# One F tile in two halves around the last scores, and the last attention tile copied tile by tile

## The chip, the cores and the metric

The kernel runs on one core of a Trainium2 chip. The metric is the device time of one execution in microseconds (us), which covers the profiled span and a little around it. All sums below are made against one profiled execution and then carried over to the median of the runs.

## The reference

A gated cross-attention block with a feed-forward layer, in fp32, over 4 batches of 512 tokens of 512 channels. The attention is across the 16 heads of one token, not across tokens.

```python
def _L0_xattn_ref(q, k, v, Wq, bq, Wk, bk, Wv, bv, Wo, bo):
    Q = (q @ Wq.T + bq).reshape(bs, sl, H, HD)      # H = 16, HD = 32
    K = (k @ Wk.T + bk).reshape(bs, sl, H, HD)
    V = (v @ Wv.T + bv).reshape(bs, sl, H, HD)
    score = jnp.einsum('bshd,bsgd->bshg', Q, K)
    weight = jax.nn.softmax(score, axis=-1)
    attn = jnp.einsum('bshg,bsgd->bshd', weight, V).reshape(bs, sl, nf)
    return attn @ Wo.T + bo
...
x = x + jnp.tanh(g_xattn[0]) * _L0_xattn_ref(_layernorm(x, axis=-1), ctx_2048, ctx_2048, ...)
x = x + jnp.tanh(g_ffn[0]) * _L0_ffn_ref(_layernorm(x, axis=-1), ...)   # x @ (weight*scale).T + bias
```

## The kernel before, in words

The 2,048 tokens are cut into 8 chunks of 256 tokens (`CHUNKS`), a chunk into 2 tiles of 128 (`TILES`). Every engine runs its own list of steps, `steps(...)`: steps 0 and 1 written out, 2 to 5 in a loop, 6, 7 and 8 written out. What an engine does in a step, and in which order, is fixed by hand in `tensor_step`, `vector_step`, `scalar_step`, `pool_step` and `sync_step`; the engines meet only through semaphores, and each works through its own list in order. Work on chunk c is called by a letter: V(c), K(c), Q(c), O(c), F(c) are the five matrix layers, score(c) and attend(c) the two small attention products, and F(5,0) is tile 0 of F(5).

Each large product is made in three parts to keep fp32 precision: every operand is split into a high part (written by ScalarE, `high`, L663) and a low part (what is left, written by VectorE, `low`, L838), and `product` (L440) adds high by high, high by low and low by high, 4 matmuls each, so 12 for a tile. A layer tile therefore waits first for the high part and, 8 matmuls later, for the low part of its input.

The change is in step 7, the last one with a chunk to attend, and touches TensorE (PE) and VectorE (DVE):

- TensorE, `tensor_step(7)`: score(7) needs q_pad, which comes back from DRAM by DMA. Then F(5,0) into the bank `score_ps[0]`, once VectorE has transposed score(7) out of that bank (`s_turned`, L545). Then O(6), F(5,1), `turn_x2` of tile (6,0) into the bank `turn_ps[0]`, attend(7). In step 8 (`last_tensor_step`): F(6,0) with the turn of (6,1) inside it, O(7), F(6,1) with the turn of (7,0), F(7,0) with the turn of (7,1), F(7,1).
- VectorE, `vector_step(7)`: `scores_turn` (L911), `softmax_a` (L923, L926), then `last_softmax_step` (L1089): the low parts of attention tiles (6,0) and (6,1) (`attn_low`, L966), `f_residual(5,0)` (L981), `softmax_b` (L934 to L941), and for each tile of chunk 6 `o_residual` (L989), `second_stats` (L852 to L863), `second_apply` (L874). The last comes back to the list once GpSimd (POOL) has made `rstd` (L1133).
- The attention result of chunk 7 lies in `attn_ps`. ScalarE (`attn_copy`, L738) and VectorE (`attn_some`, L975) copy it to `attn_t`, each 4 pieces of tile 0 and 4 of tile 1. `attn_high(7,t)` on ScalarE (L663) waits for both halves of tile t and makes its high part; `attn_low(7,t)` on VectorE waits for that. O(7) on TensorE needs both.
- GpSimd after `rstd` of both tiles adds the bias row, `x2_bias` (L1150). SyncE (SP) stores a finished tile after its `f_residual` (`save_y`, L348), in the order of its own list.

Of the kernel before, what the change touches and what calls it, by code (L numbers as in the profile page):

```python
# [66 lines left out]
def gated_attention_kernel(nc, x, ctx_t, g_attn, g_ffn, wq_t, bq, wk_t, bk, wv_t, bv, wo_t, bo,  # L67
                           wf_t, scale, bf, v_scratch, out):
    stack = ExitStack()
    with stack:  # L70
# [172 lines left out]
        def final(c):  # L243
            return isinstance(c, int) and c == CHUNKS - 1

        def late_f(c):

            return isinstance(c, int) and c == CHUNKS - 3
# [13 lines left out]
        def f_banks(c, t):  # L262

            if final(c) and t == TILES - 1:
                return last_tile
            if isinstance(c, int) and c >= CHUNKS - 3:
                return ((score_ps[t], slice(0, D)),)
            return ((acc[t], slice(0, D)),)
# [163 lines left out]
        def _(pe):  # L432
# [59 lines left out]
            def turn_x2(c, prev, tiles=range(TILES)):  # L492
                for t in tiles:
                    pe.wait_ge(n_done[1], TILES * c + t + 1)
                    prev(t)
                    turn(x2_norm, x2_turned, t)
# [4 lines left out]
            def x2_read(c):  # L501
                return lambda t: pe.wait_ge(x2_lo, TILES * c + t + 1)
# [31 lines left out]
            def f_layer(c, prev, prev_c):  # L534
# [2 lines left out]
                    bank_free(prev, prev_c, t)  # L537
                rows_layer(x2_parts, "wf", f_mm, high_ready, lambda t: pe.wait_ge(x2_lo, TILES * c + t + 1))

            def late_f_tile(c, t, within=None):  # L540

                def high_ready(t):
                    pe.wait_ge(x2_hi, TILES * c + t + 1)
                    if late_f(c):
                        pe.wait_ge(s_turned, TILES * (CHUNKS - 1) + t + 1)  # L545
                    elif final(c) and t == TILES - 1:
                        pe.wait_ge(o_out, TILES * CHUNKS)
                        pe.wait_ge(at_hi, TILES * CHUNKS)
                    else:
                        pe.wait_ge(f_out, TILES * (c - 1) + t + 1)  # L550

                def low_ready(t):
                    if within:
                        within()
                    pe.wait_ge(x2_lo, TILES * c + t + 1)
                rows_layer(x2_parts, "wf", f_mm, high_ready, low_ready, lambda t: f_banks(c, t), (t,))

            def score(c):
                pe.wait_ge(q_moved, DMA * GROUPS * (c + 1))
                pe.wait_ge(k_laid, c + 1)  # L560
                reached(pe, s_turned, 2 * c)
                pe.sem_inc(pe_passed, 1)
                for o in range(EIGHTS):
                    for pair in range(PAIRS):
                        n = GT // 2 * (pair // 2) + ROW_TOK * o + 2 * (pair % 2)
                        for r in range(2):
                            half = slice(ROWS * r, ROWS * (r + 1))
                            last = pe.matmul(  # L568
                                score_ps[r][HD * pair:HD * (pair + 1), ROWS * o:ROWS * (o + 1)],
                                k_keys[half, n:n + 2].rearrange("p s g -> p (s g)"),  # L570
                                q_pad[half, :, :, :, n:n + 2].rearrange("p t q m s -> p (t q m) s"),
                                start=True, stop=True)
                            if o == EIGHTS - 1 and pair == PAIRS - 1:
                                last.then_inc(score_mm, 1)
# [39 lines left out]
            def tensor_step(i):  # L614
                if final(i - 1):
                    return last_tensor_step(i)
                score(i)
                if final(i):
                    late_f_tile(i - 2, 0)
                    o_layer(i - 1, "v", i)  # L620
                    late_f_tile(i - 2, 1)
                    turn_x2(i - 1, x2_read(i - 2), (0,))
                    attend(i)
                    return
                if first(i):
                    q_layer(1, blocks=(1,))
                    v_layer(1)
                elif first(i - 1):
                    k_layer(2, "v", 1)
                    pe.wait_ge(w_lo, pieces_to(WO, 1))  # L630
                    o_layer(0, "k", 2)
                    q_layer(2, "o", 0)
                else:
                    o_layer(i - 1, "f", i - 2)
                    k_layer(i + 1, "o", i - 1)
                    q_layer(i + 1)
                attend(i)
                if exists(i - 1):
                    turn_x2(i - 1, x1_read(i + 1))
                    v_layer(i + 1)  # L640
                if exists(i - 1) and not late_f(i - 1):
                    if not exists(i - 2):
                        pe.wait_ge(w_lo, pieces_to(WF, 1))
                    f_layer(i - 1, "v", i + 1)
                if exists(i + 2):
                    turn_x1(i + 2, x2_read(i - 1) if exists(i - 1) else x1_read(i + 1))

            def last_tensor_step(i):

                late_f_tile(i - 2, 0, lambda: turn_x2(i - 2, x2_read(i - 3), (1,)))  # L650
                o_layer(i - 1, "o", i - 2)
                late_f_tile(i - 2, 1, lambda: turn_x2(i - 1, x2_read(i - 2), (0,)))
                late_f_tile(i - 1, 0, lambda: turn_x2(i - 1, x2_read(i - 2), (1,)))
                late_f_tile(i - 1, 1)
# [180 lines left out]
        def _(dve):  # L835
# [127 lines left out]
            def attn_low(c, t):  # L963
                dve.wait_ge(at_hi, TILES * c + t + 1)
                n = slice(P * t, P * (t + 1))
                low(at_parts(c)[:, LO, :, n], attn_t[:, :, n], at_parts(c)[:, HI, :, n]).then_inc(at_lo, 1)  # L966
# [91 lines left out]
            def vector_step(i):  # L1058
                if first(i):
                    return first_step()  # L1060
                if first(i - 1):
                    return second_step()
                if final(i - 1):
                    return last_step(i)
                scores_turn(i)
                softmax_a(i)
                if final(i):
                    return last_softmax_step(i)
                o_residual(i - 1, 0)
                softmax_b(i)  # L1070
                o_residual(i - 1, 1)
                turned_lo(xa_parts, x1_hi, x1_lo, i + 1)
                spread_first(i)
                for t in range(TILES):
                    second_stats(i - 1, t)
                    second_apply(i - 1, t)
                if exists(i + 2):
                    norm_stats(0, x_norm, i + 2)
                    norm_apply(0, x_norm, x_norm, i + 2)
                turned_lo(x2_parts, x2_hi, x2_lo, i - 1)  # L1080
                v_bias(i + 1, 0)
                v_bias(i + 1, 1)
                if not late_f(i - 1):
                    attn_low(i, 0)
                    attn_low(i, 1)
                    f_residual(i - 1, 0)
                    f_residual(i - 1, 1)

            def last_softmax_step(i):  # L1089

                attn_low(i - 1, 0)
                attn_low(i - 1, 1)
                f_residual(i - 2, 0)
                softmax_b(i)
                o_residual(i - 1, 0)
                second_stats(i - 1, 0)
                spread_first(i)
                second_apply(i - 1, 0)
                o_residual(i - 1, 1)
                second_stats(i - 1, 1)  # L1100
                turned_lo(x2_parts, x2_hi, x2_lo, i - 1, (0,))
                second_apply(i - 1, 1)
                f_residual(i - 2, 1)
                attn_some(i, 0)
                attn_some(i, 1)
                attn_low(i, 0)
                f_residual(i - 1, 0)
                attn_low(i, 1)
                turned_lo(x2_parts, x2_hi, x2_lo, i - 1, (1,))

            def last_step(i):

                o_residual(i - 1, 0)
                second_stats(i - 1, 0)
                second_apply(i - 1, 0)
                o_residual(i - 1, 1)
                second_stats(i - 1, 1)
                second_apply(i - 1, 1)
                turned_lo(x2_parts, x2_hi, x2_lo, i - 1, (0,))
                f_residual(i - 2, 1)  # L1120
                turned_lo(x2_parts, x2_hi, x2_lo, i - 1, (1,))
                f_residual(i - 1, 0)
                f_residual(i - 1, 1)
# [113 lines left out]
```

## Time and profile before

| | us |
|---|---|
| median of 3 runs | 297.7 (296.8 to 299.47) |
| profiled execution | 298.64 |
| its span, first to last instruction | 296.8 |
| TensorE busy in the span | 276.3 (93%) |
| VectorE busy | 193.4 (65%) |
| ScalarE busy | 142.4 (48%) |
| GpSimd busy | 86.5 (29%) |

Steps 7 and 8 lie from about 256.5 us to the end. A timeline row gives the start, the duration, the engine, the line, what is written from what, how many instructions are merged, and in brackets how long the engine sat idle before and what ended that. The shares of the whole span are averages: TensorE is busy almost everywhere, but the last 40 us are of another kind than the loop, since VectorE has much to do there for each matmul.

### The profile page before, as it was taken

How to read it: one execution, taken by the hardware profiler on the slowest of the kernel's cores; microseconds unless marked ns; L12 is line 12 of the kernel's file. 1: busy time of each engine (PE TensorE's matmuls, PEld its weight loads, DVE VectorE, ACT ScalarE, POOL GpSimd, SP SyncE). 2: the span in 40 equal slices, each digit the busy share in tenths (PEclk: the TensorE clock that was granted, in tenths of full speed). 3: DMA queues.
4: the chain of work that ended last, by engine and by line, in shares of the span. 5: the costliest groups of instructions: out<-in, count | busy, mean ns of one | idle time of the engine just before them, and what ended most of it. 6: DMA issues, size and time to landing. Idle time of an engine off the chain costs nothing.

```text
span 296.8 us, 8696 instructions
## 1 busy us (share of the span) xinstructions
PE 276.3 (93%) x3556; PEld 242.8 (82%) x3556; DVE 193.4 (65%) x330; ACT 142.4 (48%) x272; POOL 86.5 (29%) x80
## 2 busy tenths in 40 slices
PE   7899979398969999999999999999999999789896
PEld 7779977297957899888988899889988899578675
DVE  2595359179893687439754787459664772398974
ACT  3556625633675033672378034843288135834500
POOL 4014000032293025323180325231271237004531
PEclk9999999779997999999999999999999999999999
DMA  7994779795853662629565753748473624753102
GB/s 199 350 360 157 199 229 177 163 326 119 278 148 101 118 210 109 179 81 201 212 167 115 166 187 136 166 136 172 168 192 91 147 87 140 184 92 106 51 23 108
DMA packets 65113, 48.60 MB, mean 164 GB/s; under 512 B 36288, under 2 KB 54464, under 8 KB 65088
## 3 DMA queue, kind: packets, MB, share of 16 engines
q1 hardware_dynamic: 65088, 48.25, 59.3%
q8 instruction: 18, 0.29, 0.4%
q14 instruction: 7, 0.06, 0.1%
HBM read 31.46 MB, written 16.78 MB: 163 GB/s over the span
## 4 chain that ended last, share of the span: by engine, by line
PE 67%; DMA 11%; DVE 9%; SPq 5%; ACT 3%; issue 2%; POOL 1%; DVEq 0%; POOLq 0%; ACTq 0%
PE acc L449 55%; DMA q_scratch<-q_t 4%; PE score_ps L568 4%; PE turn_ps L483 4%; DMA late<-wv_t 3%; PE score_ps L449 2%; DMA q_pad<-q_scratch 2%; PE attn_ps L590 2%; SPq L307 1%; DMA v_scratch<-v_or_norm 1%; POOL rstd L1133 1%; DVE stats L852 1%; DVE late L975 1%; ACT late L738 1%; DVE v_or_norm L874 1%
## 5 line engine op out<-in xcount | busy, mean ns | idle before, releaser
L449 PE MATMUL acc<-ctx_parts,wk_parts 128*128 128x256 f32 x384 | 49.4, 288 | 0.5 <-ACT wk_parts L663 0.3
L449 PEld LDWEIGHTS acc<-ctx_parts,wk_parts 128*128 128x128 f32 x384 | 48.0, 195 | 1.7 <-ACT wk_parts L663 0.8
L738 ACT ACTIVATE late<-attn_ps 32x256 f32<-32x256 f32 x120 | 45.1, 376 | 6.6 <-PE attn_ps L590 3.8
L449 PE MATMUL acc<-wv_parts,ctx_parts 128*128 128x512 f32 x192 | 46.9, 399 | 1.1 <-ACT wv_parts L663 1.1
L1133 POOL TENSOR_TENSOR rstd<-var_eps,minus_half 128x1 f32<-128x1 f32 (+1 forms) x24 | 17.3, 719 | 101.8 <-DVE var_eps L863 101.8
L449 PE MATMUL acc<-xa_parts,wq_parts 128*128 128x256 f32 x384 | 46.4, 279 | 0.0
L449 PEld LDWEIGHTS acc<-xa_parts,wq_parts 128*128 128x128 f32 x384 | 45.6, 188 | 0.3
L449 PEld LDWEIGHTS acc<-wv_parts,ctx_parts 128*128 128x128 f32 x192 | 35.4, 188 | 9.1 <-issue 1.3
L449 PE MATMUL acc<-wo_parts,xa_parts 128*128 128x512 f32 x168 | 41.0, 399 | 1.0 <-ACT xa_parts L663 1.0
L449 PEld LDWEIGHTS acc<-wo_parts,xa_parts 128*128 128x128 f32 x168 | 31.1, 188 | 9.2 <-ACT xa_parts L663 1.5
L449 PE MATMUL acc<-wf_parts,x_parts 128*128 128x512 f32 (+1 forms) x132 | 32.0, 400 | 2.8 <-DVE v_or_norm L905 2.8
L449 PEld LDWEIGHTS acc<-wf_parts,x_parts 128*128 128x128 f32 x132 | 25.2, 197 | 9.1 <-issue 3.2
L1138 POOL TENSOR_TENSOR ctx_parts<-ctx_raw,ctx_parts 128x1024 fp32r<-128x1024 f32 x6 | 14.5, 2418 | 48.2 <-ACT ctx_parts L663 48.2
L1144 POOL TENSOR_TENSOR x_res<-x_res,bo_row 128x512 f32<-128x512 f32 x16 | 22.1, 1404 | 17.3 <-DVE bf_row L1033 17.3
L712 ACT ACTIVATE q_t<-acc,bq_col 128x256 f32<-128x256 f32 x32 | 13.4, 471 | 28.4 <-PE acc L449 28.4
L712 ACT ACTIVATE k_t<-acc,bk_col 128x256 f32<-128x256 f32 x32 | 13.4, 470 | 28.0 <-PE acc L449 28.0
L911 DVE STREAM_TRANSPOSE turned<-score_ps 128x512 f32<-128x512 f32 x16 | 10.5, 695 | 21.4 <-PE score_ps L568 21.4
L838 DVE TENSOR_TENSOR x_parts<-turn_ps,x_parts 128x512 fp32r<-128x512 f32 x16 | 10.5, 684 | 16.8 <-ACT x_parts L663 16.7
L693 ACT ACTIVATE probs<-probs 128x512 f32<-128x512 f32 x8 | 5.1, 632 | 33.9 <-DVE probs L926 33.9
L838 DVE TENSOR_TENSOR xa_parts<-late,xa_parts 128x512 fp32r<-128x512 f32 x14 | 9.5, 687 | 17.4 <-ACT xa_parts L663 17.4
L568 PE MATMUL score_ps<-q_pad,k_keys 64*32 64x64 f32 x1024 | 13.1, 245 | 8.4 <-DMA q_pad<-q_scratch 8.4
L874 DVE TENSOR_SCALAR x_norm<-x_norm,moments,rstd 128x512 f32<-128x512 f32 x16 | 17.6, 1140 | 5.0 <-POOL rstd L1133 5.0
(81 smaller groups left out, 371.9 us busy)
## 6 DMA issues: line engine op xcount, KB each, us to landing
ctx_raw<-ctx_t SPq DMA_DIRECT2D x8, 512.0 KB, 4.4
x_norm<-x SPq DMA_DIRECT2D x8, 512.0 KB, 5.2
k_scratch<-k_t SPq DMA_DIRECT2D x8, 512.0 KB, 2.8
k_rows<-k_scratch SPq DMA_DIRECT2D x32, 128.0 KB, 3.6
q_scratch<-q_t SPq DMA_DIRECT2D x8, 512.0 KB, 3.8
q_pad<-q_scratch SPq DMA_DIRECT2D x32, 128.0 KB, 3.2
v_scratch<-v_or_norm SPq DMA_DIRECT2D x32, 128.0 KB, 2.1
v_keys<-v_scratch SPq DMA_DIRECT2D x16, 256.0 KB, 5.3
```

What stands on the lines that cost most here:

```text
L449: last = pe.matmul(dst, left(a, k), right(b, k), start=(n == 0), stop=(n == len(terms) - 1))
L483: last = pe.transpose(turn_ps[t][:, P * k:P * (k + 1)], src[:, t, P * k:P * (k + 1)], ident[:])
L568: last = pe.matmul(score_ps[r][HD * pair:HD * (pair + 1), ROWS * o:ROWS * (o + 1)], k_keys[half, n:n + 2].rearrange("p s g -> p (s g)"), q ...
L590: last = pe.matmul(attn_ps[HD * t:HD * (t + 1), BANK * r + ROWS * eight:BANK * r + ROWS * (eight + 1)], v_keys[half, EIGHTS * t + eight, : ...
L712: nc.scalar.activation(dst[:, :, m, :], acc[m // 2][:, TOK * (m % 2):TOK * (m % 2 + 1)].rearrange("p (t n) -> p t n", t=GROUPS), ACT.Ident ...
L738: nc.scalar.activation(attn_rows(t, q), attn_block(t, q), ACT.Identity).then_inc(a_out, 1)
L838: return nc.vector.tensor_tensor(dst, src, hi.bitcast(F32), ALU.subtract)
L874: nc.vector.tensor_scalar(dst[:, t, :], src[:, t, :], moments[which][:, t, 0:1], rstd[which][:, t:t + 1], ALU.subtract, ALU.mult).then_inc ...
L911: nc.vector.transpose(by_half[:, b].rearrange("p e (s x) -> p e s x", s=2), score_ps[b][:].rearrange("p (e x s) -> p e s x", x=HT, s=2)).t ...
L1133: nc.gpsimd.tensor_tensor(rstd[which][:, t], var_eps[which][:, t], minus_half[:, t], ALU.pow).then_inc(n_rstd[which], count)
L1138: nc.gpsimd.tensor_tensor(ctx_parts[:, LO], ctx_raw[:], ctx_parts[:, HI].bitcast(F32), ALU.subtract).then_inc(ctx_lo, 1)
L1144: nc.gpsimd.tensor_tensor(x_res[:, t, :], x_res[:, t, :], bo_row[:], ALU.add).then_inc(res_biased, 1)
```

## The change

The first tile of F(5) is written to `turn_ps[0]` instead of `score_ps[0]`, in two column halves of 256: the first half ahead of score(7), the second behind it. It no longer waits for score(7) to be transposed out of its bank; the turn of (6,0), which uses `turn_ps[0]` next, waits until `f_residual(5,0)` has read it, and F(6,0), now the first to write `score_ps[0]` after score(7), takes over the wait for `s_turned`. On VectorE the low part of attention tile (6,0) moves ahead of `scores_turn`. The 8 copies of attention (7) are split: 4 for tile 0, `f_residual(5,1)`, the low part of (7,0), 4 for tile 1, the low part of (7,1), and only then `f_residual(6,0)`. The other engines' lists are unchanged.

```diff
@@ f_banks
                 return last_tile
+            if late_f(c) and t == 0:
+                return ((turn_ps[t], slice(0, D)),)
             if isinstance(c, int) and c >= CHUNKS - 3:
@@ TensorE
+            def late_f_half(c, half):
+
+                tile, cols = slice(0, P), slice(D // 2 * half, D // 2 * (half + 1))
+                if half == 0:
+                    pe.wait_ge(x2_hi, TILES * c + 1)
+                    pe.wait_ge(x2_lo, TILES * c + 1)
+                last = product(turn_ps[0][:, cols], lambda a, k: x2_parts[:, a, k, tile],
+                               lambda b, k: weights["wf"][:, b, k, cols])
+                if half == 1:
+                    last.then_inc(f_mm, 1)
+
             def late_f_tile(c, t, within=None):
                 def high_ready(t):
                     pe.wait_ge(x2_hi, TILES * c + t + 1)
-                    if late_f(c):
+                    if late_f(c) or (late_f(c - 1) and t == 0):
                         pe.wait_ge(s_turned, TILES * (CHUNKS - 1) + t + 1)
@@ tensor_step
+                if final(i):
+                    late_f_half(i - 2, 0)
                 score(i)
                 if final(i):
-                    late_f_tile(i - 2, 0)
+                    late_f_half(i - 2, 1)
                     o_layer(i - 1, "v", i)
                     late_f_tile(i - 2, 1)
+                    pe.wait_ge(f_out, TILES * (i - 2) + 1)
                     turn_x2(i - 1, x2_read(i - 2), (0,))
@@ vector_step
+                if final(i):
+                    attn_low(i - 1, 0)
                 scores_turn(i)
@@ last_softmax_step
-                attn_low(i - 1, 0)
                 attn_low(i - 1, 1)
...
+                attn_some(i, 0)
                 f_residual(i - 2, 1)
-                attn_some(i, 0)
+                attn_low(i, 0)
                 attn_some(i, 1)
-                attn_low(i, 0)
+                attn_low(i, 1)
                 f_residual(i - 1, 0)
-                attn_low(i, 1)
                 turned_lo(x2_parts, x2_hi, x2_lo, i - 1, (1,))
```

TensorE in step 7, before: score(7), then F(5,0), O(6), F(5,1) and the turn of (6,0).

```order
L449 MATMUL acc<-wv_parts,ctx_parts 128x512 x24
L568 MATMUL score_ps<-q_pad,k_keys 32x64 x64
L449 MATMUL score_ps<-wf_parts,x_parts 128x512 x12
L449 MATMUL acc<-wo_parts,xa_parts 128x512 x24
L449 MATMUL score_ps<-wf_parts,x_parts 128x512 x12
L483 MATMUL turn_ps<-ident,v_or_norm 128x128 x4
```

TensorE in step 7, now.

```order
L451 MATMUL acc<-wv_parts,ctx_parts 128x512 x24
L451 MATMUL turn_ps<-wf_parts,x_parts 128x256 x12
L581 MATMUL score_ps<-q_pad,k_keys 32x64 x64
L451 MATMUL turn_ps<-wf_parts,x_parts 128x256 x12
L451 MATMUL acc<-wo_parts,xa_parts 128x512 x24
L451 MATMUL score_ps<-wf_parts,x_parts 128x512 x12
L485 MATMUL turn_ps<-ident,v_or_norm 128x128 x4
```

The 12 matmuls of 512 columns behind the scores have become 12 of 256 columns ahead of them and 12 behind; everything else keeps its place.

VectorE from `second_apply(6,1)` (the first row) to `o_residual(7,0)` (the last), before.

```order
L874 TENSOR_SCALAR v_or_norm<-x_spare,moments,rstd 128x512 [waits n2_rstd]
L981 SCALAR_TENSOR_TENSOR late<-score_ps,tanh_g,late 128x512 [waits f_mm,x2_biased]
L975 COPY late<-attn_ps 32x4x64 [waits at_lo,attn_mm]
L975 COPY late<-attn_ps 32x4x64 x7
L838 TENSOR_TENSOR xa_parts<-late,xa_parts 128x4x128 [waits at_hi]
L981 SCALAR_TENSOR_TENSOR x_spare<-score_ps,tanh_g,x_spare 128x512 [waits f_mm,x2_biased]
L838 TENSOR_TENSOR xa_parts<-late,xa_parts 128x4x128 [waits at_hi]
L838 TENSOR_TENSOR x_parts<-turn_ps,x_parts 128x4x128 [waits x2_hi]
L989 SCALAR_TENSOR_TENSOR late<-acc,tanh_g,x_res 128x512 [waits res_biased,o_mm,y_saved0]
```

VectorE in the same stretch, now.

```order
L890 TENSOR_SCALAR v_or_norm<-x_spare,moments,rstd 128x512 [waits n2_rstd]
L991 COPY late<-attn_ps 32x4x64 [waits at_lo,attn_mm]
L991 COPY late<-attn_ps 32x4x64 x3
L997 SCALAR_TENSOR_TENSOR late<-score_ps,tanh_g,late 128x512 [waits f_mm,x2_biased]
L854 TENSOR_TENSOR xa_parts<-late,xa_parts 128x4x128 [waits at_hi]
L991 COPY late<-attn_ps 32x4x64 x4
L854 TENSOR_TENSOR xa_parts<-late,xa_parts 128x4x128 [waits at_hi]
L997 SCALAR_TENSOR_TENSOR x_spare<-score_ps,tanh_g,x_spare 128x512 [waits f_mm,x2_biased]
L854 TENSOR_TENSOR x_parts<-turn_ps,x_parts 128x4x128 [waits x2_hi]
L1005 SCALAR_TENSOR_TENSOR late<-acc,tanh_g,x_res 128x512 [waits res_biased,o_mm,y_saved0]
```

The second group of 4 copies now stands directly ahead of the low part that waits for `at_hi` of the same tile; `f_residual(6,0)`, which stood between, comes behind it.

## Rows read from the trace of the kernel before

**Rows 1.** The page: span, TensorE's line (busy us, share, instructions), stores to landing.

```profile
span 296.8 us, 8696 instructions
PE 276.3 (93%) x3556; PEld 242.8 (82%) x3556; DVE 193.4 (65%) x330; ACT 142.4 (48%) x272; POOL 86.5 (29%) x80
...
out<-late SPq DMA_DIRECT2D x13, 256.0 KB, 2.2
```

**Rows 2.** The chain of waits, 240 us to the end: start, us, what.

```profile
254.84 3.07 DMA q_pad<-q_scratch
...
287.80 1.51 DVE v_or_norm L874
289.31 0.04 issue
289.36 0.66 PE turn_ps L483 x4
```

**Rows 3.** Timeline of TensorE: start, us, line, work, idle before and its end.

```profile
258.05 1.57 PE L568 MATMUL score_ps<-q_pad,k_keys 64*32 64x64 f32 x128 [1.54 <-DMA q_pad<-q_scratch]
260.51 3.02 PE L449 MATMUL score_ps<-wf_parts,x_parts 128*128 128x512 f32 x12 [0.89 <-DVE turned L911]
263.37 5.76 PE L449 MATMUL acc<-wo_parts,xa_parts 128*128 128x512 f32 x24
...
278.27 5.87 PE L449 MATMUL acc<-wo_parts,xa_parts 128*128 128x512 f32 x24 [1.04 <-ACT xa_parts L663]
...
292.42 1.58 PE L449 MATMUL attn_ps<-wf_parts,x_parts 128*128 128x256 f32 x12
```

**Rows 4.** Timeline of VectorE around score(7).

```profile
256.54 0.69 DVE L905 TENSOR_TENSOR v_or_norm<-acc,bv_row 128x512 f32<-128x512 f32 x1 [0.91 <-PE acc L449]
259.64 1.31 DVE L911 STREAM_TRANSPOSE turned<-score_ps 128x512 f32<-128x512 f32 x2 [2.41 <-PE score_ps L568]
...
262.32 1.29 DVE L838 TENSOR_TENSOR xa_parts<-late,xa_parts 128x512 fp32r<-128x512 f32 x2
```

**Rows 5.** Timeline of VectorE, from second_apply(6,0) to o_residual(7,0).

```profile
270.40 0.55 DVE L874 TENSOR_SCALAR v_or_norm<-x_spare,moments,rstd 128x512 f32<-128x512 f32 x1 [0.51 <-POOL rstd L1133]
...
273.04 0.69 DVE L838 TENSOR_TENSOR x_parts<-turn_ps,x_parts 128x512 fp32r<-128x512 f32 x1 [0.18 <-ACT x_parts L663]
273.65 1.37 DVE L874 TENSOR_SCALAR v_or_norm<-x_spare,moments,rstd 128x512 f32<-128x512 f32 x1
274.94 0.74 DVE L981 SCALAR_TENSOR_TENSOR late<-score_ps,tanh_g,late 128x512 f32<-128x512 f32 x1
275.70 3.61 DVE L975 COPY late<-attn_ps 32x256 f32<-32x256 f32 x8
279.35 0.69 DVE L838 TENSOR_TENSOR xa_parts<-late,xa_parts 128x512 fp32r<-128x512 f32 x1
280.07 0.75 DVE L981 SCALAR_TENSOR_TENSOR x_spare<-score_ps,tanh_g,x_spare 128x512 f32<-128x512 f32 x1
...
281.94 0.74 DVE L989 SCALAR_TENSOR_TENSOR late<-acc,tanh_g,x_res 128x512 f32<-128x512 f32 x1
```

**Rows 6.** Timeline of ScalarE: high part of (6,0), then of (7,0) and (7,1).

```profile
254.08 0.64 ACT L663 ACTIVATE xa_parts<-late 128x512 fp32r<-128x512 f32 x1
...
277.59 0.63 ACT L663 ACTIVATE xa_parts<-late 128x512 fp32r<-128x512 f32 x1 [2.17 <-DVE late L975]
278.24 1.58 ACT L738 ACTIVATE late<-attn_ps 32x256 f32<-32x256 f32 x4
279.86 0.63 ACT L663 ACTIVATE xa_parts<-late 128x512 fp32r<-128x512 f32 x1
```

**Rows 7.** Timeline of GpSimd: rstd of (6,1) and x2_bias(6,0).

```profile
272.94 0.55 POOL L1133 TENSOR_TENSOR rstd<-var_eps,minus_half 128x1 f32<-128x1 f32 x1 [2.65 <-DVE var_eps L863]
273.45 1.28 POOL L1150 TENSOR_TENSOR x_spare<-x_spare,bf_row 128x512 f32<-128x512 f32 x1
```

**Rows 8.** Windows: stretch, its length, busy us by engine (instructions), TensorE's granted clock, DMA.

```profile
260.50:275.00 14.50, 14.49 (x185) 11.81 (x186) 13.19 (x25) 5.66 (x10) 3.27 (x3) 1.00 0.47 94
275.00:282.00 7.00, 5.96 (x28) 4.54 (x27) 6.69 (x15) 3.76 (x9) 3.75 (x3) 1.00 0.13 50
```

## Prediction

> **What bounds the kernel now.** I read the page first: TensorE is busy 276.3 of 296.8 us [rows 1]. That average decides nothing here, since the change lies in the last 40 us. So I read the chain of waits for that stretch, then the timelines of the four engines in it. The chain comes to TensorE with q_pad's landing, runs along TensorE through score(7), F(5,0), O(6) and F(5,1), goes over to VectorE near 273.04 [rows 5] and stays there, but for GpSimd's short `rstd` steps, until the turn of (7,1) starts at 289.36, directly behind the `second_apply` of 287.80 [rows 2]. From there matmuls lead to the end.
>
> The reader should see two things. TensorE has two gaps around score(7): 1.54 us until q_pad is there and 0.89 us until score(7) is out of its bank [rows 3], 2.43 us together. And VectorE is nearly as full as TensorE afterwards: 13.19 us of 14.50, with hardly a wait, then 6.69 us of 7.00 [rows 8]. In the second stretch TensorE has 5.96 of 7.00, so there it waits for others. The granted clock is 1.00, TensorE's upper level of 2.4 GHz, in both [rows 8]; the gaps cost no clock that could come back.
>
> **The halves of F(5,0).** V(7) ends where the 1.54 us gap begins, at 258.05 - 1.54 = 256.51. The half needs the low part of F(5)'s input; VectorE writes it ahead of the row of 256.54, so it is ready. No row shows a half into this bank, but the last rows of the kernel are 12 matmuls of the same shape: 1.58 us [rows 3]. The lower bound is half of the whole tile's 3.02 [rows 3], 1.51. I take 1.55, so the half ends near 258.06, where the scores start already. It fits the gap with nothing over: score(7) is late by 0 to 0.1, and I count 0.
>
> The second half has no wait. The scores end at 259.62, so it ends near 261.1, and O(6) starts there and not at 263.37: TensorE is 2.3 us ahead. O(6) finds its inputs: the high part of (6,0) was made at 254.08 [rows 6], its low part now comes early (next paragraph). The 5.7 us of O(6) and the 3.0 of F(5,1), a tile like F(5,0), bring TensorE to the turn of (6,0) at about 269.8 [rows 3].
>
> **VectorE ahead of the scores.** One of the two low parts of chunk 6, half of 1.29 = 0.65 us [rows 4], moves into the 2.41 us that VectorE idles before `scores_turn` [rows 4]; its input has been ready since 254.08 + 0.64. So everything behind `softmax_a` starts 0.65 us earlier. This holds only because TensorE has moved too: `o_residual(6,0)` would otherwise wait for O(6). So `second_apply(6,0)` ends at 270.95 - 0.65 = 270.3 [rows 5]. The turn of (6,0) waits for it, so TensorE gives back about 0.5 of its 2.3 us. The new wait for `f_out` there costs nothing: `f_residual(5,0)` follows the one low part left at 262.32 and is done near 263.7 (0.65 and 0.75 later); behind the turn only attend(7) is queued. The 0.18 us that VectorE waited at 273.04 [rows 5] goes. `rstd` of (6,1) follows VectorE 0.65 us earlier and with it `x2_bias` [rows 7], so `second_apply(6,1)`, 1.37 us while GpSimd's bias runs, ends at 275.02 - 0.65 = 274.4 [rows 5]. **Gain on VectorE so far: 0.65 us.**
>
> On that last row a page has something to say. The `second_apply` takes 0.55 us alone and 1.37 us behind a bias that started 0.20 earlier, at 273.45, and ended 0.29 before it [rows 5, 7]. The Trainium skill, "SBUF — State Buffer", section "Who interferes with whom", says that the two engines share one port pair as an exclusive lock and that issue order decides who blocks; this trace agrees with the blocking. What follows if the order flips is the first rival.
>
> **VectorE around the copies.** 8 copies take 3.61, so 0.45 each. The first 4 run 274.3 to 276.1 and not 275.70 to 277.5. ScalarE starts the high part 0.09 us after the fourth (277.59 against 277.50) and needs 0.63 [rows 6]; with 0.03 until VectorE goes on, 0.75 us pass from the last copy to the low part. For tile 0 this is covered: `f_residual(5,1)`, 0.76 from start to start (274.94 to 275.70), now lies between [rows 5]. The high part of (7,0) is ready at 276.8 (278.22 before), and O(7) starts there: 1.4 us earlier than 278.27 [rows 3].
>
> For tile 1 nothing lies between. The second 4 copies end near 279.3, ScalarE's own 4 (1.58 us from 276.8 [rows 6]) are done by 278.4, so the high part of (7,1) runs 279.4 to 280.05, and VectorE stands still for 0.75 us. Before, that high part came at 279.86 + 0.63 = 280.49, while VectorE was at `f_residual(6,0)` until 280.82 [rows 5, 6]: no wait. Queued behind the new stall are `f_residual(6,0)`, the low part of (6,1) and `o_residual(7,0)`, the head of the chain to the end. **Cost: 0.75 us.** Bounds: 0.63, the ScalarE row alone, and 1.05 if half of another such ScalarE row were in front of it.
>
> The other instructions are the same ones in another order: zero. SP now gets `f_residual(5,1)` 1.2 us later, its store landing about 2.2 after [rows 1], near 279; the `o_residual(7,1)` that waits for it comes later than 281.94. Nothing else stands behind it in SP's list before `f_residual(6,0)`, which is later anyway.
>
> **Sum.** -0.65 + 0.75 = +0.1 us on VectorE: `o_residual(7,0)` at 282.0 to 282.1 and not 281.94. O(7) on TensorE stalls about 0.3 us between its tiles for the high part of (7,1) (276.8 + half of 5.87 = 279.8 against 280.05) and still ends about 1 us earlier than before, to no use: the next turn waits for VectorE. From `o_residual(7,0)` to the end nothing is changed. The profiled execution goes from 298.64 to 298.7; the median of the runs lies 0.94 below that execution, so the forecast is 297.7 + 0.1 = **297.8 us**. With the bounds above (score(7) late by up to 0.1, the stall 0.63 to 1.05) the sum is 0 to +0.5.
>
> **Rivals.** (1) VectorE takes the port first. It becomes ready for `second_apply(6,1)` at 272.9 (273.04 - 0.18 - 0.65, and 0.69 for the low part), just when `rstd` ends (272.94 - 0.65 + 0.55 = 272.84); GpSimd's bias follows `rstd` without a gap. If VectorE is first, the row is 0.55 and not 1.37: 0.82 less, **297.0 us**. For: the two now come within 0.1 us of each other. Against: GpSimd needs no semaphore to go on, VectorE does. 10%.
>
> (2) TensorE's time comes through. The Trainium skill, "Perfetto Trace Analysis", sections "Identifying the Most-Contended Engine" and "Optimization Strategy", says to take the engine with the highest occupancy and close its gaps. On the page of the profile that is TensorE. If its 2.43 us reached the end, the time would be **295.3 us**; if the 1.4 us by which O(7) starts earlier did, 296.3. It decides if VectorE has slack after 275 us; the 6.69 of 7.00 speaks against it [rows 8], as does the turn 0.05 us behind `second_apply(7,1)` [rows 2]. 6%.
>
> (3) Slower: the first half pushes score(7). It stands ahead of the scores in TensorE's list, and all of VectorE's later work hangs on them. The point is q_pad's landing before the half has ended. The landing is the end of a DMA begun at 254.84 and 3.07 long, 257.91 [rows 2], against 258.06; every tenth it comes earlier, or the half runs longer, costs a tenth, up to the half's 1.58: 297.8 + 1.58 = **299.4 us**. For: no margin. Against: the half could at most fill a gap that is there now. 15%, mostly at 0.2 to 0.6.
>
> (4) The change doesn't take effect, the half starting only with the scores because of its low part: excluded but for 2% by the row of 256.54.
>
> **How the numbers follow.** Forecast 65%, rival 1 10%, rival 2 6%, rival 3 15%, rival 4 and the unforeseen 4%. The three runs spread from 296.8 to 299.47, so a median of a few moves by some tenths. I take 296.6 to 299.0: it holds the forecast, rival 1, most of rival 3, and leaves rival 2 out. A change under 1% (3.0 us) can't be told from none by a measurement of this kernel. Only rival 2 whole with some luck comes near on the fast side, rival 3 at its worst on the slow side: faster 0.05, within 1% 0.91, slower 0.04.
>
> **What would show it.** The first half between V(7) and score(7), the scores starting at 258.0 to 258.2; O(6) near 261.1; a TensorE wait of about 0.6 us for VectorE before the turn of (6,0); O(7) near 276.8; VectorE idle about 0.75 us before the low part of (7,1), released by ScalarE; `o_residual(7,0)` within 0.3 of 281.94. I am wrong if that last row is a microsecond earlier, if `second_apply(6,1)` is short, or if the scores are late.

## The result and the profile after

The changed kernel is slower: 299.75 us against 297.8 us (medians of 22 runs each), a ratio of 1.0067 with a 95% interval of 1.0044 to 1.0089. That is 2.0 us, less than 1%, but the interval leaves out 1, so it is a loss. The forecast was 297.8, with 299.0 as the upper end of the range.

The spans of the two profiled executions say the opposite, 296.2 us after and 296.8 before [rows 1]. The scores start at 255.82 and not at 258.05 [rows 3], and ahead of them the two programs differ only by the first half and the early low part. Single executions differ there by some us; one difference is the granted clock from 50 to 100 us, with a mean of 0.97 after and 0.90 before. What the change does is therefore read from the start of the scores to the start of the turn of (7,1): 31.31 us before [rows 2, 3], 32.95 after. From there to the end it is 7.4 us in both. This stretch cannot show whether the first half held the scores back, since it begins with them.

TensorE's timeline after (columns as in rows 3; the line numbers have moved by 2 in `product`):

```profile
254.14 1.59 PE L451 MATMUL turn_ps<-wf_parts,x_parts 128*128 128x256 f32 x12
255.82 1.58 PE L581 MATMUL score_ps<-q_pad,k_keys 64*32 64x64 f32 x128
257.32 1.09 PE L451 MATMUL turn_ps<-wf_parts,x_parts 128*128 128x256 f32 x7
260.13 0.75 PE L451 MATMUL turn_ps<-wf_parts,x_parts 128*128 128x256 f32 x5 [1.71 <-issue]
260.72 5.76 PE L451 MATMUL acc<-wo_parts,xa_parts 128*128 128x512 f32 x24
...
274.97 3.07 PE L451 MATMUL acc<-wo_parts,xa_parts 128*128 128x512 f32 x12 [0.38 <-ACT xa_parts L679]
279.39 3.06 PE L451 MATMUL acc<-wo_parts,xa_parts 128*128 128x512 f32 x12 [1.36 <-ACT xa_parts L679]
...
288.77 0.66 PE L485 MATMUL turn_ps<-ident,v_or_norm 128*128 128x128 f32 x4 [0.61 <-DVE v_or_norm L890]
```

The first half fills the gap ahead of the scores, as meant; the scores start 0.09 us behind its end. The second half breaks off after 7 of its 12 matmuls for 1.71 us, and the release reads "issue": the trace shows nothing that it waited for. O(7) starts early but then waits 1.36 us between its tiles, and the last turn waits 0.61 us for VectorE, where it waited for hardly anything before [rows 2].

VectorE after, from the low part of (6,0) on (as rows 4 and 5):

```profile
254.95 0.68 DVE L854 TENSOR_TENSOR xa_parts<-late,xa_parts 128x512 fp32r<-128x512 f32 x1
257.41 1.31 DVE L927 STREAM_TRANSPOSE turned<-score_ps 128x512 f32<-128x512 f32 x2 [1.78 <-PE score_ps L581]
...
260.99 0.75 DVE L997 SCALAR_TENSOR_TENSOR late<-turn_ps,tanh_g,late 128x512 f32<-128x512 f32 x1 [0.21 <-PE turn_ps L451]
...
270.99 1.38 DVE L890 TENSOR_SCALAR v_or_norm<-x_spare,moments,rstd 128x512 f32<-128x512 f32 x1
272.40 1.76 DVE L991 COPY late<-attn_ps 32x256 f32<-32x256 f32 x4
274.20 0.75 DVE L997 SCALAR_TENSOR_TENSOR late<-score_ps,tanh_g,late 128x512 f32<-128x512 f32 x1
274.95 1.83 DVE L854 TENSOR_TENSOR xa_parts<-late,xa_parts 128x512 fp32r<-128x512 f32 x1
276.81 1.80 DVE L991 COPY late<-attn_ps 32x256 f32<-32x256 f32 x4
279.37 0.69 DVE L854 TENSOR_TENSOR xa_parts<-late,xa_parts 128x512 fp32r<-128x512 f32 x1 [0.76 <-ACT xa_parts L679]
...
281.36 0.74 DVE L1005 SCALAR_TENSOR_TENSOR late<-acc,tanh_g,x_res 128x512 f32<-128x512 f32 x1
```

GpSimd in the same stretch: `x2_bias(6,1)` and the bias on the residual of chunk 7, `res_bias(7)`.

```profile
272.45 1.28 POOL L1167 TENSOR_TENSOR x_spare<-x_spare,bf_row 128x512 f32<-128x512 f32 x1 [0.36 <-DVE v_or_norm L890]
273.69 2.54 POOL L1161 TENSOR_TENSOR x_res<-x_res,bo_row 128x512 f32<-128x512 f32 x2
```

The reader should see the row of 274.95. The low part of (7,0) takes 1.83 us; it took 0.69 before [rows 5]. It begins with the second of GpSimd's two `res_bias` instructions (half of the row's 2.54 is 1.27, and 273.69 + 1.27 = 274.96) and ends 0.55 after that one's end at 276.23. And at 279.37 the predicted wait for ScalarE stands, 0.76.

From the start of the scores to `o_residual(7,0)` it is 25.54 us after and 23.89 before [rows 3, 5]: +1.65. The terms: early low part -0.65, wait for the second half +0.21, long low part +1.14, stall +0.76, together +1.46; the other 0.2 are tenths, 0.12 of them between `second_apply(6,1)` and the copies, which now follow it directly.

### The profile page after: what moved, and what is told of

Same layout as the page of the kernel before. It is cut to its first block, busy times and chain, and to the rows that moved or that the text cites. A ratio compares the mean times of both kernels' runs of the same rounds, so it can differ in the third digit from the quotient of the medians.

```text
span 296.2 us, 8720 instructions
## 1 busy us (share of the span) xinstructions
PE 275.0 (93%) x3568; PEld 241.4 (81%) x3568; DVE 195.4 (66%) x330; ACT 142.7 (48%) x272; POOL 86.5 (29%) x80
## 4 chain that ended last, share of the span: by engine, by line
PE 68%; DVE 11%; DMA 8%; SPq 5%; issue 3%; ACT 2%; POOL 1%; DVEq 0%; ACTq 0%; POOLq 0%
PE acc L451 55%; PE turn_ps L485 4%; PE score_ps L581 4%; DMA late<-wv_t 3%; DMA q_scratch<-q_t 3%; PE attn_ps L603 2%; DVE stats L868 1%; PE score_ps L451 1%; SPq L309 1%; DMA v_scratch<-v_or_norm 1%; POOL rstd L1150 1%; DVE late L991 1%; DVE x_parts L854 1%; PE turn_ps L451 1%; DMA q_pad<-q_scratch 1%
## 5 line engine op out<-in xcount | busy, mean ns | idle before, releaser
L451 PE MATMUL acc<-ctx_parts,wk_parts 128*128 128x256 f32 x384 | 48.1, 283 | 0.8 <-ACT wk_parts L679 0.7
L451 PEld LDWEIGHTS acc<-ctx_parts,wk_parts 128*128 128x128 f32 x384 | 46.6, 189 | 2.3 <-ACT wk_parts L679 1.1
L451 PE MATMUL acc<-xa_parts,wq_parts 128*128 128x256 f32 x384 | 47.4, 283 | 0.0
L451 PEld LDWEIGHTS acc<-xa_parts,wq_parts 128*128 128x128 f32 x384 | 46.6, 192 | 0.4 <-issue 0.2
L451 PE MATMUL acc<-wf_parts,x_parts 128*128 128x512 f32 (+1 forms) x132 | 30.4, 386 | 3.4 <-DVE v_or_norm L921 3.4
L451 PEld LDWEIGHTS acc<-wf_parts,x_parts 128*128 128x128 f32 x132 | 24.0, 188 | 9.3 <-issue 3.8
L854 DVE TENSOR_TENSOR xa_parts<-late,xa_parts 128x512 fp32r<-128x512 f32 x14 | 10.8, 770 | 17.9 <-ACT xa_parts L679 17.9
L742 ACT ACTIVATE k_keys<-k_rows 128x1024 f32<-128x1024 f32 x8 | 16.4, 2055 | 6.1 <-DMA k_rows<-k_scratch 6.1
```

The source lines that it names most:

```text
L451: last = pe.matmul(dst, left(a, k), right(b, k), start=(n == 0), stop=(n == len(terms) - 1))
L742: nc.scalar.activation(k_keys[:].rearrange("p n (m q) -> p n m q", q=QH), k_rows[:].rearrange("p q m n -> p n m q"), ACT.Identity).then_in ...
L854: return nc.vector.tensor_tensor(dst, src, hi.bitcast(F32), ALU.subtract)
```

## The experiments

All ratios are to the kernel before, run beside on the same chip. "Stretch" is from the start of the scores to that of the turn of (7,1), in the one profiled execution.

| kernel | ratio (95% interval) | stretch us |
|---|---|---|
| before | 1 | 31.31 |
| changed | 1.0067 (1.0044 to 1.0089) | 32.95 |
| changed, again | 1.0055 (1.0022 to 1.0087) | 33.22 |
| changed, VectorE's old order | 0.9975 (0.994 to 1.001) | 30.90 |
| before, only VectorE's new order | 1.0058 (1.0027 to 1.0089) | 33.39 |
| changed, `res_bias(7)` after the low part | 0.9988 (0.9954 to 1.0021) | 31.81 |
| changed, old order, bias steps moved | 0.9953 (0.9928 to 0.9977) | 31.32 |
| before, bias steps moved | 0.9959 (0.9931 to 0.9988) | 30.22 |

Two theories stood. The VectorE theory: the loss lies around the copies, in the long low part and the stall. The TensorE theory: it lies in the 1.71 us gap, or in scores pushed back by the first half.

**The changed kernel again**, no edit.

> The changed kernel itself, a second profile beside the kernel before on the same chip. VectorE theory (the loss lies between the copies and o_residual(7,0)): from the start of the scores to o_residual(7,0) again 25.5 us (23.9 before), with the low part of (7,0) at 1.8 us and a stall of 0.76 before the low part of (7,1); time about 1.6 to 2.0 us over before. TensorE theory (the gap of 1.7 us inside the second half of F(5,0) is what costs): the gap is there again, and runs with a longer gap are longer by as much.

The low part of (7,0) again takes 1.83 us, the stall 0.76, and the gap in the second half is there at the same place, 1.75 us. Here the scores waited 0.27 us for q_pad after the half had ended: the half did not push them. So the long low part, the stall and the gap are no accident of one execution.

**VectorE's old order in the changed kernel.**

```diff
-                attn_some(i, 0)
                 f_residual(i - 2, 1)
-                attn_low(i, 0)
+                attn_some(i, 0)
                 attn_some(i, 1)
-                attn_low(i, 1)
+                attn_low(i, 0)
                 f_residual(i - 1, 0)
+                attn_low(i, 1)
```

> The changed kernel with VectorE's old order around the copies (f_residual(5,1), 8 copies, low (7,0), f_residual(6,0), low (7,1)); the halves of F(5,0), their bank and the early low part of (6,0) stay. VectorE theory: the low part of (7,0) is back at 0.7 us, no stall before (7,1), scores to o_residual(7,0) about 23.5 us, time 0.3 to 0.5 us under before (ratio to before 0.998 to 0.999). TensorE theory, or scores pushed by the first half: the time stays 1.5 to 2 us over before (ratio 1.005 to 1.007).

```profile
275.07 3.60 DVE L991 COPY late<-attn_ps 32x256 f32<-32x256 f32 x8
278.70 0.69 DVE L854 TENSOR_TENSOR xa_parts<-late,xa_parts 128x512 fp32r<-128x512 f32 x1
```

The low part is back at 0.69, there is no stall, and scores to `o_residual(7,0)` is 23.48 us. The gap in the second half is there with 1.71 us all the same, and the time is not over that of before: 0.9975. So the gap does not cost what the change lost, and neither does the first half ahead of the scores, which is there too.

**Only VectorE's new order, in the kernel before** (the reverse edit).

> The kernel before with nothing but VectorE's new order around the copies; TensorE's list and the place of the low part of (6,0) are those of before. VectorE theory: a stall of 0.75 us before the low part of (7,1), the low part of (7,0) at 1.8 to 1.9 us while GpSimd's bias runs, together 1.9 us over before (ratio 1.006). TensorE theory: 0.75 us over before at most (ratio 1.000 to 1.003).

```profile
276.54 1.83 DVE L838 TENSOR_TENSOR xa_parts<-late,xa_parts 128x512 fp32r<-128x512 f32 x1
278.40 1.81 DVE L975 COPY late<-attn_ps 32x256 f32<-32x256 f32 x4
280.96 0.69 DVE L838 TENSOR_TENSOR xa_parts<-late,xa_parts 128x512 fp32r<-128x512 f32 x1 [0.76 <-ACT xa_parts L663]
```

With TensorE's list untouched a loss of the same size is here: 1.0058, against 1.0055 for the changed kernel beside it. The VectorE theory holds, the TensorE theory falls as the cause of the loss.

**GpSimd's bias behind the low part**, in the changed kernel.

```diff
+                    if final(i):
+                        pool.wait_ge(at_lo, TILES * i + 1)
                     res_bias(i)
```

> The changed kernel with GpSimd's bias on the residual of chunk 7 held back until the low part of (7,0) is done, so that the two no longer run at once. If GpSimd's bias is what makes that low part 1.83 us: it takes 0.7, and the time falls by 1.1 us against the changed kernel (0.5 to 0.9 us over before, ratio 1.002 to 1.003). If something else makes it long (ScalarE reading the same bank, the new place): it stays at 1.8 and the time at 1.6 to 2.0 over before.

```profile
276.31 0.69 DVE L854 TENSOR_TENSOR xa_parts<-late,xa_parts 128x512 fp32r<-128x512 f32 x1
277.03 1.80 DVE L991 COPY late<-attn_ps 32x256 f32<-32x256 f32 x4
279.59 0.69 DVE L854 TENSOR_TENSOR xa_parts<-late,xa_parts 128x512 fp32r<-128x512 f32 x1 [0.76 <-ACT xa_parts L679]
...
277.08 2.54 POOL L1161 TENSOR_TENSOR x_res<-x_res,bo_row 128x512 f32<-128x512 f32 x2 [1.98 <-DVE xa_parts L854]
```

Same instruction, same place in VectorE's list, GpSimd idle for 1.98 us: 0.69. The 1.14 us were GpSimd's bias. They were not ScalarE's four copies out of `attn_ps`, which began with the low part in both kernels (274.94 after, 276.30 here, 1.58 us each). The stall of 0.76 is still there. The stretch is 1.14 us shorter than in the changed kernel and 0.50 longer than before, as expected. The median fell by 1.3 us against the changed kernel beside it (299.23 to 297.89); the ratio of 0.9988 lies under the expected 1.002 to 1.003, whose lower end its interval (0.9954 to 1.0021) just takes in.

**The bias steps moved out of VectorE's way**, first with VectorE's old order in the changed kernel, then in the kernel before. `x2_bias` of chunks 6 and 7 starts after both `second_apply`, `x2_bias(6,1)` after the last low part.

```diff
+                if final(i):
+                    x2_bias(i - 1, (0,), TILES)
+                    res_bias(i)
+                    pool.wait_ge(at_lo, TILES * CHUNKS)
+                    x2_bias(i - 1, (1,))
+                    return
                 if exists(i - 1):
-                    x2_bias(i - 1)
+                    x2_bias(i - 1, done=TILES if final(i - 1) else None)
```

> The changed kernel with VectorE's old order around the copies, and GpSimd's bias steps moved out of VectorE's way: x2_bias(6,0) and x2_bias(7,0) start only when second_apply of both tiles of the chunk is done, x2_bias(6,1) only after the low parts of chunk 7. If GpSimd's bias is what makes second_apply of the second tile 1.4 and 1.5 us long: both fall to 0.55, o_residual(7,0) comes 0.8 earlier and the turn of (7,1) another 0.95; time 2.0 to 2.3 us under before (ratio 0.992 to 0.993). If something else makes them long: they keep their length and the time is that of the run with the old VectorE order, ratio 0.997 to 0.998, or worse by what the held steps cost.

> The kernel before with nothing but the same moves of GpSimd's bias steps: no halves of F(5,0), no early low part. Port theory: both second_apply at 0.55; the first gain is cut short where VectorE then waits for TensorE, at most 0.8, the second 0.95 in full; ratio 0.994 to 0.995, so that what the halves and the early low part add to the run beside it is 0.4 to 0.5 us. If the bias is not the cause: ratio 1.000.

In the kernel before with this edit alone, `second_apply` of (6,1) and (7,1):

```profile
273.59 0.54 DVE L874 TENSOR_SCALAR v_or_norm<-x_spare,moments,rstd 128x512 f32<-128x512 f32 x1
...
286.91 0.55 DVE L874 TENSOR_SCALAR v_or_norm<-late,moments,rstd 128x512 f32<-128x512 f32 x1 [0.67 <-POOL rstd L1133]
```

They took 1.37 [rows 5] and 1.51 [rows 2]. Both kernels beat the one before, at 0.9953 and 0.9959, but by less than the 0.992 to 0.993 and the 0.994 to 0.995 expected. In the second the list reached `o_residual(7,0)` 0.83 us earlier, as forecast; the turn of (7,1) gained only another 0.26 and not 0.95, because TensorE was still at the matmuls ahead of it (it starts at 288.20 without a wait, and `second_apply(7,1)` is done at 287.46). That the first kernel is hardly better than the second was not expected either. Its one profile shows a cause; whether its other executions had it is not on record. TensorE around the gap, and windows with the granted clock (the column of 0.55 and 0.59):

```profile
259.94 1.04 PE L451 MATMUL turn_ps<-wf_parts,x_parts 128*128 128x256 f32 x5 [1.72 <-issue]
260.78 7.06 PE L451 MATMUL acc<-wo_parts,xa_parts 128*128 128x512 f32 x24
```

```profile
258.00:260.00 2.00, 0.28 (x3) 0.19 (x3) 1.97 (x6) 0.78 (x2) 0.00 (x0) 1.00 0.02 4
260.00:262.00 2.00, 2.00 (x8) 1.77 (x8) 1.49 (x3) 0.63 (x1) 0.00 (x0) 0.55 0.38 62
262.00:264.00 2.00, 2.00 (x7) 1.56 (x6) 1.90 (x4) 0.00 (x0) 0.00 (x0) 0.59 1.03 161
```

Behind the gap the granted clock was 0.55 and 0.59, near its lower level of 1.2 GHz. O(6) took 7.06 us instead of 5.76, and VectorE waited 0.78 us for it. The four other profiles with a gap of 1.7 us at this place show a granted clock of 1.00 after it.

**The place in the instruction stream.** The 12 matmuls at the very start of TensorE's list (`WARM`), which compute nothing that is used, are made fewer or more. The run with 4 has the bias steps in place; the others have them moved. All have VectorE's old order.

```diff
-WARM = (12,)
+WARM = (4,)     # then 20, 28, 6, 8
```

> The changed kernel with VectorE's old order, and 8 of the 12 matmuls that keep the clock at the very start left out (they compute nothing that is used), so that every later TensorE instruction stands 16 places earlier in the instruction stream (a weight load and a matmul each). If the 1.7 us gap in the second half of F(5,0) is the supply of instructions at a fixed place of the stream: it comes 8 matmuls later, behind the third matmul of O(6); f_residual(5,0) no longer waits 0.2 us for the half, and the time falls by 0.2 at most. If it is a wait or a conflict of these matmuls: the gap stays behind the seventh matmul of the half.

> The kernel with GpSimd's bias steps moved and VectorE's old order, with 20 instead of 12 matmuls keeping the clock at the very start, so that every later TensorE instruction stands 16 places later in the stream. There the 1.7 us gap in the second half of F(5,0) was followed by 3 us at a granted clock of 0.55 to 0.59, which made O(6) 1.3 us longer. If the place in the stream makes the gap: it goes away or moves, and where none follows the scores the clock stays at 1.00 in O(6) and o_residual(6,0) doesn't wait; time 0.7 to 1.0 us less (ratio to before 0.992 to 0.993), unless the gap comes back at a place that costs as much. If the gap belongs to these matmuls: ratio 0.995 again.

> The same with 28 matmuls at the start, 32 places later in the stream. Place theory: again another place of the gap, or none, so the two runs differ from each other; without a gap behind the scores ratio 0.992 to 0.993. If the gap belongs to these matmuls: behind the seventh of the second half again, ratio 0.995.

> The kernel with GpSimd's bias steps moved and VectorE's old order, with 6 instead of 12 matmuls at the very start. In the runs with 12, 20 and 28 the gap stood 7 matmuls behind the scores' end, 9 before it and 25 before it: 2 places for each matmul added. By that the place is now 19 matmuls behind the scores' end, behind the seventh of O(6). TensorE gets there about 4.7 us after the scores' start, and the gap has ended 4.3 us after it so far: no gap there, the clock 1.00 in O(6), no wait at o_residual(6,0); then 0.7 to 1.0 us less than with 12 (ratio to before 0.992 to 0.993), unless another place of the stream now stalls early in the program, as a 3.1 us one did with 4 matmuls. If the place is no fixed one: the gap is behind the seventh matmul of the half again.

> The same with 8 matmuls at the very start: by two places for each matmul the gap stands 15 matmuls behind the scores' end, behind the third of O(6), about 3.7 us after the scores' start, and is at most 0.6 us long. f_residual(5,0) does not wait. Time between that with 12 and 0.8 us less (ratio 0.992 to 0.995), with the same reservation.

TensorE at the scores with 20, 28 and 8 of them:

```profile
256.04 1.47 PE L581 MATMUL score_ps<-q_pad,k_keys 64*32 64x64 f32 x119 [0.19 <-DMA q_pad<-q_scratch]
260.61 0.35 PE L581 MATMUL score_ps<-q_pad,k_keys 64*32 64x64 f32 x9 [3.10 <-issue]
260.89 2.75 PE L451 MATMUL turn_ps<-wf_parts,x_parts 128*128 128x256 f32 x12
263.44 6.26 PE L451 MATMUL acc<-wo_parts,xa_parts 128*128 128x512 f32 x24
```

```profile
258.86 1.29 PE L581 MATMUL score_ps<-q_pad,k_keys 64*32 64x64 f32 x103 [0.21 <-DMA q_pad<-q_scratch]
262.78 0.48 PE L581 MATMUL score_ps<-q_pad,k_keys 64*32 64x64 f32 x25 [2.63 <-issue]
```

```profile
260.23 0.85 PE L451 MATMUL acc<-wo_parts,xa_parts 128*128 128x512 f32 x3
261.39 5.16 PE L451 MATMUL acc<-wo_parts,xa_parts 128*128 128x512 f32 x21 [0.30 <-issue]
```

| at the start | gap stands | gap us | ratio (95% interval) |
|---|---|---|---|
| 28 | 25 matmuls before the scores' end | 2.63 | 1.0079 (1.0049 to 1.0109) |
| 20 | 9 before it | 3.10 | 1.0014 (0.9981 to 1.0047) |
| 12 | 7 behind it | 1.72 | 0.9953 (0.9928 to 0.9977) |
| 8 | 15 behind it (third of O(6)) | 0.30 | 0.9957 (0.9933 to 0.9981) |
| 6 | none there | | 0.9938 (0.9906 to 0.9969) |

The gap moves by exactly two matmuls for each one added or left out, in four kernels, so it belongs to a place of the stream and not to F(5,0), its bank or its operands. The factor of two is in the trace: the 12 appear as 24 pairs of weight load and matmul. I had counted one in the first of these runs (4 instead of 12: 1.0012, 0.9974 to 1.005) and so looked behind the third matmul of O(6), where nothing was; by two it would stand behind the eleventh, and there TensorE was not held up. Instead gaps stood in step 0: one of 3.06 us two matmuls behind score(0) with 4, one of 3.73 two matmuls before its end with 6, again two places for each matmul. With 8 the same count puts it six before the end, and no gap shows there: such a place need not hold TensorE up.

With 20 the clock fell as well. Behind the gap of 3.10 us the second half took 2.75 us (1.68 with 8) and O(6) 6.26, and the granted clock was 0.78, 0.50 and 0.86 in the three windows of 2 us from 260 on. Behind the 2.63 us with 28 it was 1.00.

Not every wait that reads "issue" is such a gap. With 4 at the start:

```profile
268.14 0.55 DVE L890 TENSOR_SCALAR v_or_norm<-x_spare,moments,rstd 128x512 f32<-128x512 f32 x1 [0.51 <-POOL rstd L1150]
268.79 0.63 PE L485 MATMUL turn_ps<-ident,v_or_norm 128*128 128x128 f32 x4 [0.68 <-issue]
```

The turn of (6,0) starts 0.10 us after the `second_apply` that it needs has ended (268.69). The same 0.10 stands there with 6 and with 28, behind an "issue" of 0.67 and 0.73, so this one stays with the turn whatever the shift: it is the wait for VectorE of about 0.6 that the prediction named.

The expected ratios of the last two runs (0.992 to 0.993 with 6, 0.992 to 0.995 with 8) were not met in the median, though the stretch is 29.45 us with 6 and 29.38 with 8, 1.9 under that of before. With 6 the gap in step 0 stands against it; with 8 I have no such cause. The stretch of one profiled execution is not the whole time.

## Why the prediction was wrong

**The halves: right in place, wrong in one detail.** The first half ran between V(7) and the scores, 1.59 us long, and did not push them in the executions where q_pad's landing ended the wait. In the profiled execution of the changed kernel no such wait stands ahead of them, so there it may have pushed them; by how much no row shows. "The second half has no wait" was true of semaphores and false of time: 1.71 us without a releaser, 0.21 of it on VectorE. So TensorE was 0.42 us ahead at O(6) (4.90 us after the start of the scores, 5.32 before) and not 2.3. Where no gap follows the scores, with 4 and 6 matmuls at the start, it was 2.3 and 2.2 us ahead, as forecast. By the count of matmuls, the place of the gap lies behind O(6)'s seventh matmul in the kernel before, some 7 us after the start of its scores, and no gap shows there.

**The early low part: right.** It ran at 254.95 in idle time, and with VectorE's old order the list reached `o_residual(7,0)` 0.41 us earlier, about the 0.65 less the 0.21.

**The stall before the low part of (7,1): right**, 0.76 measured against 0.75.

**The step that failed: "The other instructions are the same ones in another order: zero."** The low part of (7,0) moved from 279.35 [rows 5], half a microsecond after GpSimd's bias work of that stretch, into the middle of it, and took 1.83 us instead of 0.69. GpSimd's row before, ending at 278.84:

```profile
276.34 2.50 POOL L1144 TENSOR_TENSOR x_res<-x_res,bo_row 128x512 f32<-128x512 f32 x2
```

I had the same collision in hand for `second_apply(6,1)`, made it a rival in the direction of a gain, and did not ask of the moved instructions what GpSimd would be doing at their new time. The page I had named, the Trainium skill's "SBUF — State Buffer", section "Who interferes with whom", says it outright: a VectorE instruction with two inputs in SBUF contends with a GpSimd instruction that reads SBUF. The low part reads `late` and `xa_parts`, both in SBUF. The runs agree: 1.83 with the bias running, 0.69 without. VectorE's copies out of `attn_ps` did not grow: the first four ran beside the bias (272.40 to 274.16) at 0.44 each, against 0.45 before.

With this term (+1.14) the sum of +0.1 would have been about +1.2, which is 298.9, a tenth inside the range. The wait of 0.21 and some tenths bring it to the +1.65 of the profiled executions, 299.35 and outside. The other 0.3 of the 2.0 us is within the interval of the ratio (1.3 to 2.7 us). The prediction also held that a change under 1% can't be told from none on this kernel; with 22 runs of each it can.

**Rivals:** VectorE going first did not happen (`second_apply(6,1)` takes 1.38 us again); TensorE's lead, where there was one, was gone before the turn of (7,1), as predicted; the slower rival came true in sign, by another mechanism.

## What to carry to other kernels

When instructions are put in another order, look up for each of them what the other engines do at its new time, not only what it waits for: in these runs the low part, with two SBUF operands, took 1.83 us instead of 0.69 beside a GpSimd bias, and `second_apply` 1.37 to 1.51 instead of 0.55, while copies out of PSUM kept their time. Splitting a run of copies so that a consumer can start early cost the producer's own engine a stall of 0.76 us, because the last piece had nothing behind it to cover the round trip. And where a kernel's time moves without a wait that explains it, look for "issue" gaps. First ask whether the engine starts just behind the end of something that it needs; if not, see whether the gap moves with the instructions ahead of it.

## What the runs showed of the hardware

The gaps of 1.7 us and more in TensorE's work belong to places of the instruction stream, and all those seen stood inside or just behind the 128 short matmuls of a score. In the changed kernel one packet of the instruction queue moved 1.8 us after the scores had started (window 257.6 to 257.8, share of 16 engines' time):

```profile
q8 instruction: 1, 0.02, 28.8%
```

The 256 instructions of the scores take 1.58 us. In the kernel before, a packet moves 1.6 us after its scores' start too (window 259.6 to 259.8), and no gap follows. That the matmuls waited for this packet is a reading that was not tried by itself: they went on only at 260.13, 2.3 us after it.

Between 12 and 28 of the unused matmuls at the start of the program, its ratio went from 0.9953 to 1.0079, more than any other of these edits moved it. Not all of that is the place of the code: the stretch grew by 0.94 us (31.32 to 32.26) of some 3.7, and the added matmuls also put off the first product, from 6.82 to 9.68 us in the profiles. How the rest divides is open.
